# Indirect writes of one batch strewn over the next slot instead of in one burst, and its rows scaled and stored at that slot's end

## What is computed

```python
scores = jnp.where(j >= i, scores, -jnp.inf)       # first layer
attn = jax.nn.softmax(scores, axis=-1)
out = jnp.einsum('bhij,bhjd->bhid', attn, v)
...
return out @ w_out + b_out
# after each attention: layernorm(x + attention); each token then goes to TOP_K = 2 experts,
# its result added back, and a layernorm again
def _layernorm(x, axis=-1, eps=1e-05):
    m = jnp.mean(x, axis=axis, keepdims=True)
    v = jnp.var(x, axis=axis, keepdims=True)
    return (x - m) / jnp.sqrt(v + eps)
```

## Time and profile before

| | us |
|---|---|
| median of 3 runs | 1810.16 |
| fastest and slowest of them | 1808.2, 1813.23 |
| the profiled execution | 1827.05 |
| its span in the profile | 1825.3 |
| PE busy in it | 1480.0 |

### The profile page before, as it was taken

One profiled execution on the slowest core, in us unless ns is written; L12 is line 12 of the kernel. 1 busy time (PEld: TensorE's weight loads), 2 busy tenths in 40 slices (PEclk: granted clock), 3 DMA queues, 4 the chain that ended last, 5 costly groups with the idle time before them and its releaser, 6 DMA issues.

```text
span 1825.3 us, 31302 instructions
## 1 busy us (share of the span) xinstructions
PE 1480.0 (81%) x10329; PEld 968.2 (53%) x10330; DVE 957.6 (52%) x3689; ACT 693.6 (38%) x957; POOL 498.8 (27%) x422
## 2 busy tenths in 40 slices
PE   3688888888978828999649999999998629999970
PEld 1244454444544525666425555555555429999970
DVE  3657766767667531111175767776843344444424
ACT  1143443433434511110017566666676402222222
POOL 4121323234132431121210122222121234444430
PEclk8788797787878868999869999999998759999995
DMA  6735346343350306352234446435626324444448
GB/s 160 190 89 96 81 94 136 77 97 83 88 107 15 105 15 199 94 136 73 46 70 93 94 96 134 111 77 111 130 61 177 131 65 70 70 72 72 70 72 254
DMA packets 122238, 182.88 MB, mean 100 GB/s; under 512 B 17111, under 2 KB 104561, under 8 KB 114432
## 3 DMA queue, kind: packets, MB, share of 16 engines
q1 hardware_dynamic: 98336, 151.84, 34.2%
q0 software_dynamic: 21504, 27.76, 9.2%
q10 hardware_dynamic: 2272, 1.67, 0.3%
HBM read 111.47 MB, written 77.02 MB: 103 GB/s over the span
## 4 chain that ended last, share of the span: by engine, by line
PE 56%; DVE 17%; issue 7%; DMA 5%; ACT 4%; POOL 1%; another core or an unknown queue 1%; SPq 1%; DVEq 0%; ACTq 0%; POOLq 0%
PE ST L1796 7%; PE shared L1808 7%; PE ST L702 6%; PE OT L720 6%; PE ST L1262 6%; DVE scratch L1094 4%; PE shared L746 3%; PE OT L1270 3%; PE shared L1270 3%; PE shared L794 2%; PE shared L1457 2%; DMA x_in<-sum 2%; PE shared L811 2%; PE shared L763 2%; PE shared L801 2%
## 5 line engine op out<-in xcount | busy, mean ns | idle before, releaser
L835 ACT ACTIVATE arena<-ST 128x1024 f32<-128x1024 f32 x416 | 414.6, 1025 | 333.3 <-PE ST L702 316.5
L1094 DVE CUSTOM_DVE_ANT_0 scratch<-shared,mask 128x512 bf16<-128x512 f32 (+3 forms) x512 | 229.1, 487 | 119.0 <-PE shared L811 102.1
L702 PE MATMUL ST<-arena 96*128 96x256 bf16 (+2 forms) x1792 | 258.3, 282 | 15.3 <-DMA arena<-qk_parts 13.2
L720 PE MATMUL OT<-arena,v_aug 128*32 128x256 f32 (+1 forms) x3584 | 261.5, 394 | 4.1 <-POOL arena L1162 2.7
L702 PEld LDWEIGHTS ST<-arena 96*128 96x128 bf16 (+1 forms) x1792 | 161.8, 104 | 119.8 <-issue 50.9
L811 PE MATMUL shared<-arena 96*128 96x512 bf16 (+3 forms) x512 | 133.0, 340 | 54.7 <-DVE mx L1094 26.4
L1162 POOL TENSOR_SCALAR_AFFINE_SELECT arena<-arena 128x512 f32<-128x512 f32 (+1 forms) x96 | 78.6, 818 | 306.8 <-ACT arena L835 306.8
L1905 POOL DMA_INDIRECT sum<-arena,block_to_row x72 | 111.3, 1546 | 169.2 <-ACT arena L1859 157.7
L720 PEld LDWEIGHTS OT<-arena,v_aug 128*32 128x32 f32 x3584 | 86.5, 112 | 120.8 <-issue 69.7
L1808 PE MATMUL shared<-arena 128*128 x576 | 136.1, 379 | 0.0
L811 PEld LDWEIGHTS shared<-arena 96*128 96x128 bf16 x512 | 45.6, 105 | 136.7 <-issue 60.9
(11 more groups left out here) (208 smaller groups left out, 2387.4 us busy)
## 6 DMA issues: line engine op xcount, KB each, us to landing
arena<-qk_parts SPq DMA_DIRECT2D x224, 128.0 KB, 7.1
qk_parts<-qk_src SPq DMA_DIRECT2D x64, 384.0 KB, 2.6
arena<-qk_parts SPq DMA_DIRECT2D x32, 384.0 KB, 4.5
block_rows<-slot_x SPq DMA_DIRECT2D x72, 130.0 KB
arena<-qk_parts SPq DMA_DIRECT2D x32, 256.0 KB, 5.3
sum<-x_out SPq DMA_DIRECT2D x16, 512.0 KB, 2.9
arena<-in_experts_inter SPq DMA_DIRECT2D x7, 1024.0 KB, 5.0
arena<-in_experts_out SPq DMA_DIRECT2D x7, 1024.0 KB, 9.4
```

The lines of the kernel that those rows point to most:

```text
L702: mm = pe.matmul(ST[n % 2][:, i * 256 + at:i * 256 + at + nq], K[par][0:rows, h, kb * P:(kb + 1) * P], Q[par][0:rows, h, q0:q0 + nq], star ...
L720: mm = pe.matmul(OT[32 * i:32 * i + 32, q0:q0 + nq], v_aug[par][:, kb, g * GH + i, :], PT[n % RING][:, i, at:at + nq], start=(u == 0), sto ...
L835: act.activation(PT[n % RING][:, :, :], ST[n % 2][:, :].rearrange("p (h n) -> p h n", h=GH), func, scale=ATT_SCALE).then_inc(L["exp"], 1)
L1094: taken = dve.tensor_tensor_reduce(out=junk[n % 2][:, at:at + m], in0=bank[:, at:at + m], in1=mask[:, 0:m], scale=1.0, scalar=LOW, op0=ALU ...
```

## The change

The scatters get the name `s3` and take batch s-3: those of a batch are issued in the slot behind the one that routes it. A new function `among` lays them singly among the steps of the first part of the slot, by the steps' weights. `xs` and `sv` of the same batch go to the end of that slot; `xp` stays where it was. In the ninth slot the scatters of batch s-3 come first among its steps, with their scaling and store behind them, then those of the last batch as `s2`, in one row as before. A batch below zero is passed over.

```diff
+def among(steps, few, weight):
+    whole = sum(weight.get(step, 0) for step, _ in steps)
+    out, at, done = [], 0, 0
+    for step in steps:
+        out.append(step)
+        at += weight.get(step[0], 0)
+        while done < len(few) and at * (len(few) + 1) >= whole * (done + 1):
+            out.append(few[done])
+            done += 1
+    return out + few[done:]
...
-    save = ([("xs", 3), ("sv", 3)] if route else []) + ([("xp", 0)] if attn else [])
+    save = [("xs", 3), ("sv", 3)] if route else []
+    residual = [("xp", 0)] if attn else []
...
-    scatter = [("sc", i) for i in range(2 * TB)] if route else []
+    scatter = [("s3", i) for i in range(2 * TB)] if route else []
+    last_scatter = [("s2", i) for i in range(2 * TB)] if kind == "ninth" else []
...
     if not prep:
-        others = y + norm + save + rows + route_1 + route_2 + route_3 + scatter + last_save
+        others = (among(y + norm + residual + rows + route_1, scatter, cost) + route_2 + route_3 + save
+                  + last_scatter + last_save)
...
-        rest = ([("v", 0), ("v", 1)] + start + y + norm[0:NORM_FIRST] + load[1:] + norm[NORM_FIRST:] + save + load[0:1]
-                + rows + route_1 + halves[0] + route_2 + route_3 + scatter + halves[1])
+        rest = (among([("v", 0), ("v", 1)] + start + y + norm[0:NORM_FIRST] + load[1:] + norm[NORM_FIRST:] + residual
+                      + load[0:1] + rows + route_1, scatter, WEIGHT)
+                + halves[0] + route_2 + route_3 + halves[1] + save)
...
-            others = (y + project[0:1] + norm[0:6] + project[1:3] + norm[6:12] + project[3:4] + norm[12:18] + project[4:6] + norm[18:] + save + load
-                      + project[6:] + mixed(combine, rows + route_1 + route_2 + route_3) + scatter)
+            others = (among(y + project[0:1] + norm[0:6] + project[1:3] + norm[6:12] + project[3:4] + norm[12:18]
+                            + project[4:6] + norm[18:] + residual + load + project[6:], scatter, cost)
+                      + mixed(combine, rows + route_1 + route_2 + route_3) + save)
...
-                    elif step == "sc":
-                        k, par, half = turn.batch(2)
+                    elif step in ("s2", "s3"):
+                        k, par, half = turn.batch(int(step[1]))
+                        if k < 0:
+                            continue
```

More of the change, by code:

```diff
@@ L209, in spread_out @@
     route_3 = (before_sums + [("ps", 0)] + pieces("l3", n3)) if route else []
-    scatter = [("sc", i) for i in range(2 * TB)] if route else []
+    scatter = [("s3", i) for i in range(2 * TB)] if route else []
+    last_scatter = [("s2", i) for i in range(2 * TB)] if kind == "ninth" else []
+    cost = COST[causal]
     combine = pieces("cb", N_COMBINE)
@@ L246, in spread_out @@
         if not route:
-            start = save
+            start = residual
             n = PROJECT_FIRST[kind]
@@ L262, in spread_out @@
     n_units = NG * per_group
-    cost = COST[causal]
     total, at = sum(cost.get(step, 0) for step, _ in others), 0
```

## The result

The changed kernel took 1827.52 us (median of 20 runs) against 1810.24 us for the kernel before: 17.3 us or 0.9% slower, ratio 1.0089 with a 95% interval of 1.0068 to 1.0109. I had forecast 1806 and a range of 1784 to 1815. The sign was wrong.

The account below looks back on a forecast made before the run. PE was taken as the bound, busy 1480.0 of 1825.3 us with 56% of the chain. Terms +0.5, -1.6, -1.5 and -1.5 made about -4 from 1810.2, so 1806, range 1784 to 1815.

Parts of the forecast that it names:

- part 1: Eight scatters become singles, half a slot to a slot later: POOL's own time unchanged, sums released earlier worth 0.
- Part 3: First-layer slot ends: late signals around scatter bursts might vanish; bounds 0 to -29 us, taken as 0, plus -1.5 estimated.
- Rival B: Faster: late signals belong to every execution and to bursts alone; 25.7 us less, 1784 to 1790, up to 1795; chance 0.32.
- the hint that the single DMAs of the second layer's blocks show none: Second layer's blocks: 72 single indirect DMAs show no late signals, hinting that spacing matters; no size of its own.
- Part 1, the eighth slot: First layer's eighth slot: singles delay masks, scaling leaves ACT; from -1.7 to +2.5 us, taken as +0.5.
- single number 5: Scatter standing directly before the mask PE waits for in the first layer's eighth slot: at most +1.24 us.
- Part 2: Scaling and store go to the slot's end: -1.6 us in the second layer's eighth slot, scaling hidden at body slot ends.
- The load of x_in: Second layer's body slots: the store leaves SP's queue ahead of this load; -1.5 us, range -3 to +1.5.
- the two terms: Second layer: -1.6 us for scaling leaving the eighth slot and -1.5 us for the load of x_in.
- The rule on slow scatters: Skill's rule: singles among DVE work cost POOL about 2 us more each, total about 1810; set aside on the trace.
- The slower rival: C: a single scatter delays engine signals mid slot as a burst does; 1817.5 us, range 1814 to 1824; chance 0.15.

Follow-up runs that it names:

- e9: Kernel before with each first-layer scatter replaced by its semaphore step, so no scatter DMA there; 1808.51 us against 1807.67 for the kernel before.
- e8: Kernel before without the first layer's scatters and with POOL's two split sums held until DVE's chain is through; 1791.09 us against 1807.67 before.
- e7: Changed kernel with POOL's two sums held and each first-layer single scatter behind one mask step; 1816.49 us against 1807.67 for the kernel before.
- c_after: Changed kernel run again without edit, signals late; 1823.67 us against 1831.1 for the kernel before, ratio 0.9943.
- e5: Changed kernel with POOL's last two split sums of a first-layer slot held until DVE's four-step chain is through; 1804.12 us against 1831.1 before.
- c_after2: Changed kernel run once more without edit, signals on time; 1833.61 us against 1807.67 for the kernel before, ratio 1.0133.
- e3: Kernel before with only scaling and store moved to the slot's end, scatters in their old row of eight; 1824.36 us against 1826.18 before.
- e1: Changed kernel with the first layer put back as before, second layer as changed; 1822.08 us against 1826.18 for the kernel before, ratio 0.9973.

## Why the prediction was wrong

**The step that failed** is in part 1: "What was queued behind the burst ... comes about 3 us earlier, but what it feeds is used half a slot later: 0." I asked who uses the sums' result, and not whom they run beside. The burst was a hold, and what it held back were two POOL sums that now run beside DVE's two-input steps and stretch them. The price, with signals on time: 17.4 us (e9 less e8), and 1833.61 - 1816.49 = 17.1 us between the changed kernel and e7, which also places its singles otherwise. The term of 0 should have been about +17. Part of it is seen directly: PE's stop grows from 0.56 to 2.03 us in each of five slots, and PE's waits for o_nat (us in all, times, longest) from 6.1 us in e8 to 13.8 in e9, 7.7 us:
```profile
PE shared L811 <- DVE o_nat L912: 6.1, 8, 2.7
```
```profile
PE shared L811 <- DVE o_nat L912: 13.8, 8, 3.1
```
The profiled execution of e9 is 1803.9 - 1788.9 = 15.0 us longer than that of e8. PE is busy for 1473.8 - 1469.4 = 4.4 us more of it, on the same 10329 matmuls, and idle for 10.6 us more. So most of this difference is idle time of PE, and only 4.4 us are longer work, which is where a lower granted clock shows. The single slot of 0.80 against 0.86 would tell otherwise; e9's first two body slots have the same stop at 0.91 and 0.88. The runs say the same. The clock moves one kernel by more than the change does: e9's runs go from 1800.0 us at a mean clock of 0.888 to 1827.6 at 0.870. At like clocks (0.885 to 0.888) e9 is still 11.4 to 15.0 us above e8. In two other pairs PE's longer busy time is the larger part: 15.3 of 23.8 us between the profiles of c_after and e5, 16.0 of 23.2 between those of c_after2 and e7. Whether the stops bring the clock down there, no run shows, as none changed the clock alone. It is not even with one stop: the same slot of c_after, with the 2.03 us, lasted 73.0 us at 0.88:
```profile
374.29:447.31 73.02, 61.28 (x462) 33.62 (x462) 54.96 (x225) 31.29 (x42) 24.53 (x25) 0.88 0.44 101
```

The Trainium skill ("SBUF — State Buffer", section "SBUF: two separate sides") says that a DVE instruction with two SBUF inputs and a GpSimd instruction that reads SBUF share an exclusive port pair, and whoever starts first holds it for its whole length. The trace agrees to 0.15 us: a step that can only run once the sum is through would end 0.19 us (L1125) and 0.69 us (L1089) behind it, its own length, and they ended 0.06 and 0.55 us behind it. In the prediction I weighed this section's warning on scatters, which the trace had already put aside, and passed over this half of it.

**Part 3**, the late signals: I took their 17.1 us as belonging to the profiled execution, for the coincidence with 16.9. The number was right for the runs that counted, the reason wrong: they stand in all three profiles of the kernel before, two of them from groups in which every run took over 1820 us, and the measurement was made with signals on time. Calling one side from a coincidence of two numbers was luck where it came out right. Rival B's mechanism may exist: c_after is 7.4 us faster than before where signals are late, against B's 25.7, and e5, in which the sums are held, is 27.0 us faster. That is the whole change and the hold together, so it is near B's price but doesn't show it by itself; and signals are still late in both. The table also has more "remote" waits than I counted: besides the nine of L840 and L922, two of L835 (7.3 us) and one of L1492 (4.0 us). And the hint that the single DMAs of the second layer's blocks show none was a wrong reading, as the last section says.

**Part 1, the eighth slot.** Taken at +0.5, bound +2.5. PE's wait for the mask rose from 0.86 to 2.07 us, 1.2 us, as the bound for single number 5 said, and ACT's absence gave nothing back:
```profile
621.16 0.99 POOL L1193 DMA_INDIRECT slot_x<-x_out,row_to  x1
622.17 1.10 POOL L1181 TENSOR_SCALAR_AFFINE_SELECT arena<-arena 128x1024 f32<-128x1024 f32 x1
...
623.33 0.65 PE L739 MATMUL OT<-arena,v_aug 128*32 128x128 f32 x16 [2.07 <-POOL arena L1181]
```
**Part 2** held in the main. The second layer's eighth slot gave 3.36 - 1.78 = 1.6 us as forecast; the scaling at the slot's end costs nothing that shows with signals late (e3, three times below before), and 0.2 us a slot by the timeline with signals on time. The load of x_in: DVE's six waits for it went from 30.2 to 25.7 us in all, and the second layer's part as a whole is a gain of 4.1 and 5.7 us (e1, twice, signals late), where the two terms made 3.1.

**The rule on slow scatters** changed nothing, as said: they average 984 (first layer) and 1037 ns (second) among DVE's work, against 999 and 994.
```profile
L1660 POOL DMA_INDIRECT slot_x<-x_out,row_to x64 | 66.4, 1037 | 157.5 <-DVE keep L1571 144.2
...
L1193 POOL DMA_INDIRECT slot_x<-x_out,row_to x64 | 63.0, 984 | 38.4 <-DVE row_to L990 24.4 <-issue 13.8
```
**The slower rival** (C) had the sign but not the cause: in the profile that was measured no signal was late. 

**Open.** With signals on time the change costs 17.3 us in one measurement and 25.9 in another, and the sums explain 17. The other 9 (e7 against before) may be the singles before the masks, what the late scaling does beyond its 0.2 us a slot, or the clock; no run with signals on time parts them. For the same reason I can't say that e5 beats the kernel before where signals are on time: it does where they are late, by 1.4 to 1.9%.

## What to carry to other kernels

A long instruction that holds a queue can be doing another engine a service: before moving it, list not only who waits for what stood behind it, but what that will run beside once it is released, and look there for two-input DVE steps against POOL steps that read SBUF. Where such a hold is needed, make it a wait of its own, which here gave 17.4 us (e9 against e8) and 19.6 us (c_after against e5). Before giving the rest of a loss to the granted clock, add up PE's busy and idle time over the whole execution: one slot picked out can tell the opposite. And where a profile's own time lies 1% above the runs' median, find out which of its waits belong to the difference before pricing an edit by them.

## What the runs showed of the hardware that I had not expected

- Signals of PE, ACT and DVE come several us late beside rows of indirect DMAs, in some groups of runs and in none of others, with the same kernel: medians of 1808 and 1810 us on time, 1826 to 1841 us late. The trace's records of semaphore updates, which none of the rows shows, have late ones in the second layer's blocks too: in each profile of the late kind more than 60 come over 0.8 us behind the end of their instruction, and in those with signals on time none. No "remote" wait follows from them there, and for that I had called them absent.
- A DVE step of 0.19 us became 1.16 us beside one POOL sum.
- Ten runs of one kernel (e9), beside each other on one chip, spread over 27.6 us with their mean granted clock: 1800.0 us at 0.888, 1827.6 us at 0.870.
